# Adding each step's probabilities in two halves, and moving sums, projections and value products in the order

## The reference

```python
q = (x @ wq_w.T + wq_b).reshape(b, t, H, HD)
k1, v1 = (x @ wk_w.T + wk_b), (x @ wv_w.T + wv_b)      # one head of 32
scores = jnp.einsum('bqhd,bkd->bhqk', q, k1) / jnp.sqrt(jnp.float32(HD))
weights = jax.nn.softmax(jnp.where(causal, scores, -jnp.inf), axis=-1)
attn = jnp.einsum('bhqk,bkd->bqhd', weights, v1).reshape(b, t, H * HD)
x = _layernorm(x + (attn @ wo_w.T + wo_b))
x_scale = FP8_MAX / jnp.maximum(jnp.max(jnp.abs(x2)), EPS)   # w_scale alike
out = clip(x2 * x_scale) @ clip(weight * w_scale) * (1.0 / (x_scale * w_scale))
x = _layernorm(x + out)
```

## Time and profile before

| what | value |
|---|---|
| median of three runs | 2414.62 us |
| profiled execution | 2413.82 us |
| its span (first to last instruction) | 2411.7 us |
| mean granted TensorE clock | 0.991 |
| attention, batch 0 to last value product | 417.8 to about 1989 us |
| batches 1 to 19, no projection | 422.6 to 528.3 us |
| batches 20 to 271 | 528.3 to 1987 us |

### The profile page before, as it was taken

How to read it: one execution, slowest core, us unless ns; L and a number is a source line. 1 busy time by engine, 2 the same in 40 slices (tenths; PEclk the granted TensorE clock), 3 DMA queues, 4 the chain that set the end, 5 groups by cost and what they waited for, 6 DMA issues and landing times.

```text
span 2411.7 us, 34838 instructions
## 1 busy us (share of the span) xinstructions
PE 2338.3 (97%) x13933; PEld 1484.1 (62%) x13933; DVE 1809.0 (75%) x1466; ACT 1346.0 (56%) x1459; POOL 640.1 (27%) x381
## 2 busy tenths in 40 slices
PE   8999998899999999999999999999999998999998
PEld 6887776345555555555555555555555556888887
DVE  6455447798889888889899988988888885444444
ACT  3433334777777777777777777777777772000000
POOL 1000002011323222232222222322223222666663
PEclk9999999999999999999999999999999999999999
DMA  7777875211311222121211122122212222222221
GB/s 279 258 266 258 285 261 198 41 36 47 78 45 45 64 55 60 45 67 45 67 45 45 54 69 56 45 54 58 67 45 58 61 71 107 87 87 89 93 87 61
DMA packets 160249, 231.60 MB, mean 96 GB/s; under 512 B 9614, under 2 KB 109934, under 8 KB 158318
## 3 DMA queue, kind: packets, MB, share of 16 engines
q1 hardware_dynamic: 136494, 178.27, 25.5%
q10 hardware_dynamic: 23616, 51.39, 5.7%
HBM read 140.50 MB, written 89.13 MB: 95 GB/s over the span
## 4 chain that ended last, share of the span: by engine, by line
PE 71%; DVE 5%; ACT 3%; issue 2%; POOL 1%; DMA 0%; ACTq 0%; DVEq 0%; POOLq 0%
PE bank L1372 20%; PE bank L1384 18%; PE bank L1447 14%; PE bank L1357 13%; ACT prob L821 3%; DVE acc L1118 2%; PE bank L1394 2%; POOL prob L663 1%; PE bank L1437 1%; PE bank L1402 1%; DVE acc L1114 1%; DVE r_den L1073 1%; DVE r_parts L1077 0%; DVE res L1090 0%; DMA wf<-wf_sim_d 0%
## 5 line engine op out<-in xcount | busy, mean ns | idle before, releaser
L821 ACT ACTIVATE prob<-bank 128x1024 f32<-128x1024 f32 x1088 | 1055.8, 1023 | 410.2 <-PE bank L1372 390.2
L1118 DVE TENSOR_TENSOR acc<-acc,prob 128x2048 f32<-128x2048 f32 x420 | 961.1, 2288 | 58.1 <-ACT prob L821 35.1
L1372 PE MATMUL bank<-q_st,keys 98*128 98x512 f32 x2176 | 646.8, 416 | 16.6 <-ACT prob L821 13.2
L1372 PEld LDWEIGHTS bank<-q_st,keys 98*128 98x128 f32 x2176 | 376.2, 189 | 352.7 <-ACT prob L821 259.7
L1384 PE MATMUL bank<-prob,v_t 128*32 128x512 f32 x4352 | 525.8, 601 | 0.0
L663 POOL TENSOR_SCALAR_AFFINE_SELECT prob<-prob 128x1024 f32<-128x1024 f32 x128 | 206.4, 1636 | 743.2 <-ACT prob L821 743.2
L1384 PEld LDWEIGHTS bank<-prob,v_t 128*32 128x32 f32 x4352 | 114.0, 109 | 263.4 <-issue 251.6
L1114 DVE TENSOR_TENSOR acc<-prob 128x2048 f32<-128x2048 f32 x60 | 137.6, 2293 | 118.4 <-ACT prob L821 87.9
L634 POOL TENSOR_SCALAR moments<-moments 128x1 f32<-128x1 f32 x64 | 66.8, 1044 | 596.7 <-DVE moments L878 568.9
L1357 PE MATMUL bank<-wo_hi,att_hi 128*128 128x512 f32 x512 | 209.0, 408 | 14.4 <-issue 11.3
L852 ACT ACTIVATE xs_hi<-bank 128x1024 fp32r<-128x1024 f32 x32 | 32.9, 1029 | 336.3 <-DVE y L883 328.3
(11 more groups left out here) (131 smaller groups left out, 2435.6 us busy)
## 6 DMA issues: line engine op xcount, KB each, us to landing
q_st<-q_hi_d SPq DMA_DIRECT2D x128, 256.0 KB
q_hi_d<-part_hi ACTq DMA_DIRECT2D x64, 256.0 KB, 2.2
q_lo_d<-part_lo ACTq DMA_DIRECT2D x64, 256.0 KB, 2.8
x_row<-x SPq DMA_DIRECT2D x32, 512.0 KB, 3.9
xb_d<-x_row SPq DMA_DIRECT2D x32, 512.0 KB, 3.9
q_st<-q_lo_d SPq DMA_DIRECT2D x64, 256.0 KB
res<-xb_d SPq DMA_DIRECT2D x32, 512.0 KB, 5.5
x_d<-res SPq DMA_DIRECT2D x32, 512.0 KB, 2.7
```

What stands on the lines that cost most here:

```text
L821: nc.scalar.activation(prob[:, s % SLOTS, 2 * p:2 * p + 2], bank[:, 2 * p:2 * p + 2], ACT.Exp, scale=SCALE).then_inc(p_done, 1)
L1118: nc.vector.tensor_tensor(acc[:, n % 2], acc[:, n % 2], new, ALU.add).then_inc(acc_done, 1)
L1372: last = nc.tensor.matmul(bank[:, g].rearrange("p (a n) -> p a n", n=P), keys[:, k // QT, k % QT * P:(k % QT + 1) * P], queries[:, :, g], ...
```

## The change

VectorE's add of a step becomes two adds of 128x1024, each behind its own exponential, and `acc_done` counts two a step. The residual sums stand ahead of the adds of their step. In `places` the projection ranges, sums and what follows them come two steps (one batch) later, with four ranges of three batches for the next to last pair. Statistics go to the first group that begins at or after SUM1, and deviation, scaling and maximum are placed from there. In a batch without a slice of projection, the value product of step 2u-2 stands between the two scores.

```diff
@@ -311,29 +311,36 @@
         LAST_GROUP = len(groups) - 1
         WF_ORDER = (6, 7, 4, 5, 0, 1, 2, 3)
 
+        SPLIT, HALF0, HALF0_END, SUM0, HALF1, HALF1_END, SUM1, DEVIATION, SCALE_ROW, LARGEST, STATISTICS = range(11)
+
         def places(q):
 
 
 
             p, second = divmod(q, 2)
             if p < len(pairs) - 2:
-                names = (13, 22, 28, 28, 30, 38, 38, 39, 44, 45) if second else (4, 6, 12, 12, 14, 20, 20, 22, 27, 28)
+                names = (13, 24, 30, 30, 32, 40, 40, 41, 46, 47) if second else (4, 8, 14, 14, 16, 22, 22, 23, 28, 29)
                 base = (p + 1) * PAIR
             elif p == len(pairs) - 2:
-                names = (11, 18, 22, 22, 24, 30, 30, 31, END, END) if second else (4, 6, 10, 10, 12, 16, 16, 18, 22, 23)
+                names = (11, 20, 24, 24, 26, 30, 30, 31, END, END) if second else (4, 8, 12, 12, 14, 18, 18, 19, 23, 24)
                 base = (p + 1) * PAIR
             else:
                 names = (END,) * 10 if second else (31,) + (END,) * 9
                 base = p * PAIR
-            return [base + at for at in names]
+            at = [base + at for at in names]
+            statistics = at[SUM1]
+            if p < len(pairs) - 2:
+                statistics = min(first for first in begins if first >= at[SUM1])
+                at[DEVIATION], at[SCALE_ROW] = statistics + 1, statistics + 6
+                at[LARGEST] = min([first for first in begins if 0 <= first - statistics - 7 <= 4] + [statistics + 7])
+            return at + [statistics]
 
         def at_place(name):
 
             return {places(q)[name]: q for q in range(TILES) if places(q)[name] < STEPS}
 
-        SPLIT, HALF0, HALF0_END, SUM0, HALF1, HALF1_END, SUM1, DEVIATION, SCALE_ROW, LARGEST = range(10)
         split_at, sum0_at, sum1_at, deviation_at = at_place(SPLIT), at_place(SUM0), at_place(SUM1), at_place(DEVIATION)
-        scale_at, largest_at = at_place(SCALE_ROW), at_place(LARGEST)
+        scale_at, largest_at, statistics_at = at_place(SCALE_ROW), at_place(LARGEST), at_place(STATISTICS)
         fillers = {}
         for q in range(LAST_A):
             at = places(q)
@@ -815,7 +822,7 @@
             for s in range(STEPS):
                 if s < STEPS:
                     act.wait_ge(pv_done, s + 1)
-                    act.wait_ge(acc_done, s + 1)
+                    act.wait_ge(acc_done, 2 * (s + 1))
                     for p in range(2):
                         act.wait_ge(s_done, 2 * s + p + 2)
                         nc.scalar.activation(prob[:, s % SLOTS, 2 * p:2 * p + 2], bank[:, 2 * p:2 * p + 2], ACT.Exp, scale=SCALE).then_inc(p_done, 1)
@@ -885,7 +892,7 @@
             dve.sem_inc(wf_tile_read, 1)
             dve.sem_inc(norm_read, 2)
             dve.sem_inc(lo_cut, 2)
-            dve.sem_inc(acc_done, SLOTS)
+            dve.sem_inc(acc_done, 2 * SLOTS)
             dve.sem_inc(att_ready, 2)
             dve.sem_inc(t_lo, 2)
             dve.sem_inc(f_read, 4)
@@ -1100,6 +1107,10 @@
                 nc.vector.tensor_tensor(att_lo[q % 2][:], att[:, q % TILES_KEPT], att_hi[q % 2][:].bitcast(F32), ALU.subtract).then_inc(att_cut, 1)
 
             for s in range(STEPS):
+                if s in sum0_at:
+                    add_residual(sum0_at[s], 0)
+                if s in sum1_at:
+                    add_residual(sum1_at[s], 1)
                 if s < STEPS:
                     n, t = steps[s]
                     new = prob[:, s % SLOTS]
@@ -1107,27 +1118,27 @@
                         dve.wait_ge(den_done, n + 1)
                     if t == 0 and lengths[n] == 1:
                         dve.wait_ge(masked, 2 * n + 2)
-                        nc.vector.tensor_copy(acc[:, n % 2], new).then_inc(acc_done, 1)
+                        nc.vector.tensor_copy(acc[:, n % 2], new).then_inc(acc_done, 2)
                     elif t == 1:
                         dve.wait_ge(masked, 2 * n + 2)
-                        dve.wait_ge(p_done, 2 * s + 4)
-                        nc.vector.tensor_tensor(acc[:, n % 2], prob[:, (s - 1) % SLOTS], new, ALU.add).then_inc(acc_done, 2)
+                        for p in range(2):
+                            heads = slice(2 * p, 2 * p + 2)
+                            dve.wait_ge(p_done, 2 * s + p + 3)
+                            nc.vector.tensor_tensor(acc[:, n % 2, heads], prob[:, (s - 1) % SLOTS, heads], new[:, heads], ALU.add).then_inc(acc_done, 2 * p + 1)
                     elif t > 1:
-                        dve.wait_ge(p_done, 2 * s + 4)
-                        dve.wait_ge(acc_done, s + SLOTS)
-                        nc.vector.tensor_tensor(acc[:, n % 2], acc[:, n % 2], new, ALU.add).then_inc(acc_done, 1)
-                if s in sum0_at:
-                    add_residual(sum0_at[s], 0)
-                if s in sum1_at:
-                    add_residual(sum1_at[s], 1)
+                        for p in range(2):
+                            heads = slice(2 * p, 2 * p + 2)
+                            dve.wait_ge(p_done, 2 * s + p + 3)
+                            dve.wait_ge(acc_done, 2 * (s + SLOTS) + p - 1)
+                            nc.vector.tensor_tensor(acc[:, n % 2, heads], acc[:, n % 2, heads], new[:, heads], ALU.add).then_inc(acc_done, 1)
                 if s % 2 == 0 and s // 2 in group_of_den:
                     invert(group_of_den[s // 2])
                 if s % 2 == 0 and s // 2 - 1 in group_of_den:
                     normalise_group(group_of_den[s // 2 - 1])
                 if s in split_at:
                     lower_attended(split_at[s])
-                if s in sum1_at:
-                    q = sum1_at[s]
+                if s in statistics_at:
+                    q = statistics_at[s]
                     dve.wait_ge(y_read, 2 * q + 2)
                     moments_of(res[:, q % 2], stats[:, q % 2], moments[:, q % 2], ln1, q * LN)
                 if s in largest_at:
@@ -1388,7 +1399,7 @@
             def denominators(n):
 
                 pe.wait_ge(att_ready, n + 2)
-                pe.wait_ge(acc_done, begins[n] + lengths[n] + SLOTS)
+                pe.wait_ge(acc_done, 2 * (begins[n] + lengths[n] + SLOTS))
                 for g in range(HG):
                     for c in range(QT):
                         last = nc.tensor.matmul(bank[c * HD:(c + 1) * HD, DEN_BANK, 0:P], head_col[:, g], acc[:, n % 2, g, c * P:(c + 1) * P],
@@ -1414,9 +1425,13 @@
             for u in range(BATCHES):
                 scores(2 * u)
                 between(u)
+                single = u >= 1 and u not in fillers
+                if single:
+                    weigh_values(2 * u - 2)
                 scores(2 * u + 1)
+                if u >= 1 and not single:
+                    weigh_values(2 * u - 2)
                 if u >= 1:
-                    weigh_values(2 * u - 2)
                     weigh_values(2 * u - 1)
             weigh_values(STEPS - 2)
             weigh_values(STEPS - 1)
```

## The result

The changed kernel takes 2397.89 us (median of four runs, 2397.3 to 2399.34), the kernel before 2414.32 in the same comparison. The ratio is 0.9932, 95% interval 0.9921 to 0.9944: 16.4 us faster. Forecast were 2387.5 us and 27 us less, in a range of 2374 to 2406. The sign is right and the time is inside the range, but the gain is 0.6 of what was forecast, and the reasons are further from the forecast than the number is.

The account below looks back on a forecast made before the run. Instruction order bounds batches 1 to 19; later TensorE is full, with stalls on VectorE's late results. Terms -13 - 0.5 - 13 - 5 + 3 + 1.5 = -27 take 2413.8 to 2386.8 us, 2387.5 as median; range 2374 to 2406.

Parts of the forecast that it names:

- (a): Batches 1 to 20 and 271: value product ahead of the second scores fills TensorE's wait; -13 us, and -0.5 for batch 271.
- the sum by VectorE's work: Batches 1 to 20: VectorE may set the rate; 94 us of work plus start and waits gives 98 to 101.
- The check by TensorE alone: Batches 1 to 20 by TensorE only: 16 at 4.43, four with denominators at 5.25, 2 for the clock; 94 us.
- (b): Adds in halves: 1.14 us each, 2.28 a step against 2.38; in the projection part the gain costs and gives nothing.
- rival E: Slower: a half add costs over 1.33 us, VectorE bounds the projection part, about 2440 us; chance 0.11.
- (c): Projections one batch later: `att_lo` is ready in time, 14 stalls ahead of projections go; -13 us.
- (d): Residual ahead of the adds, next half a batch later: four waits for residuals and two smaller ones go; -5 us.
- (e): Costs: eight projection halves end in batches with denominators, so inverses come late for spreads, +3 us; projection slices fall differently, +1.5.
- Slices: Projection matmuls spread differently over batches of the next to last pair and three more denominator batches; +1.5 us.
- A: The forecast as summed holds: 2376 to 2398 us; chance 0.58.
- B: Smaller gain: halves start 1.22 us apart, or waiting residuals leave VectorE short; 2397 to 2408 us; chance 0.17.
- B's second part: Projection part: up to 1.7 us of waiting at 56 residuals leaves VectorE short, so stalls partly return.

Follow-up runs that it names:

- places_only: Kernel before with later projections, sums ahead of adds and moved statistics, but whole adds and the old order of value products: 2418.9 us, ratio 1.0010.
- whole_adds: Changed kernel with whole adds again in place of half adds: 2411.4 us, ratio 0.9977.
- pool_later: Changed kernel with GpSimd's first statistic, and that tile's scaling and maximum, two steps later, behind the mask of step 68: 2390.1 us, ratio 0.9902.
- sum_by_den: Changed kernel with the residual sum behind the adds again in steps where a group's inverse is due: 2386.8 us, ratio 0.9887.
- halves_only: Kernel before with only the adds split in halves: 2403.4 us, ratio 0.9937.

## Why the prediction was right or wrong, point by point

**What bounds the kernel: right.** Order in the plain part, a full TensorE with short stalls in the rest. The floor of 5.35 for six matmuls stayed.

**(a) The value product: right in size, with a term that wasn't in the sum.** Forecast -13 for batches 1 to 20, measured -12.6; plain batch forecast 4.43, measured 4.5. 6.9 us come with the product alone and 12.6 with the half adds too, since half adds let VectorE keep up with the faster batches, as the sum by VectorE's work said. But some 3.1 of the 12.6 us are clock: that the first batch's 7.52 us "stays" was wrong, and the second slow stretch was left to the range (up to 2 us). Without them the gain would be 9.5 us, still in the -8 to -18. The check by TensorE alone has a slip: 4.43 + 1.15 is 5.58 and not 5.25 for a batch with denominators (measured 5.38 to 5.65), and it counts the four batches with a spread as plain, which took 5.27 to 5.78. The forecast didn't rest on it.

**(b) Half adds: the price right, the worth wrong.** 1.13 us from start to start against 1.14 taken; rival E, a half that costs over 1.33 us, is dead. By the page VectorE: DVE Perf Modes of the Trainium skill (section The TRN2 errata — SBUF-src ops pay a fixed extra latency per instruction) each half should last 1.22 us (an estimate), and it does (L1133, 1221 ns); but VectorE's busy time rose by 16.7 us and not by 75, since halves that follow each other overlap. The step that failed is the sentence that a gain there "costs and gives nothing", since VectorE isn't the bound. It priced throughput only. The halves take 0.92 us off the wait at the head of each chain of residual, cut and inverse, and TensorE waited at the end of those chains: -10.1 us in batches 21 to 270, alone, and 15 without GpSimd's first use.

**(c) and (d), stalls that go: right that they go, wrong to whom they belong.** No wait ahead of a projection is left after, as forecast, and long time in batches without denominators or spread fell from 15.8 to 1.6 us. But most of it had two cures in the same change. Places and sums without halves remove these stalls too (places_only has about 1.4 us of them left) and lose as much elsewhere, by the waits shown for whole_adds and GpSimd's pause. The forecast counted -18 for them and had nothing against them but (e).

**(e) Costs: the mechanism right, the size too small.** The sum ahead of the adds makes the inverse late where a half ends in a batch with denominators. Forecast eight cases, 0.7 each at most, taken as 3; there are nine, at 0.87, 7.8 us in all. The reason given for halving it, that in many the add is the second step of a group and late anyway, was wrong: that add waits for its sum as well. Slices: +1.5 forecast, +2.1 by the usual lengths.

**What the prediction didn't have.** GpSimd's first use, 5.5 us. The text let GpSimd's root move along without a cost and looked at SP's queue but not at GpSimd's own, where the next group's mask now stood behind the first statistic. The trace of before held it: there the configuration change is issued at 578.2 and the first statistic starts at 584.96, with nothing queued behind it. And 2.8 us behind the last value product (422.7 us before, 425.5 after). There the last denominators wait 1.26 us for an add, where they waited 0.09. The rest is TensorE's clock in the following 70 us, and that is not the change's doing. Busy time of these 70 us, after, before and in pool_later, whose code there is that of after:

```profile
1969.03:2039.03 70.00, 58.80 (x296) 46.83 (x289) 42.43 (x55) 16.70 (x17) 20.28 (x16) 0.90 0.29 108
```
```profile
1987.06:2057.06 70.00, 59.60 (x308) 47.66 (x301) 42.73 (x53) 16.17 (x16) 22.88 (x18) 0.93 0.30 111
```
```profile
1961.37:2031.37 70.00, 58.66 (x304) 46.93 (x297) 43.60 (x56) 16.68 (x17) 22.07 (x18) 0.93 0.31 113
```

pool_later has the same wait of 1.27 us, but the clock of before, and takes 423.6 us to the end (sum_by_den too). So about 0.9 of the 2.8 us are the change's.

Together: -27 forecast; +4.8 for (e), +5.5 for GpSimd, +0.6 for slices, +2.8 at the end and +1.2 at the start make -12.1; the stalls that went were 21.2 us and not 18, which makes -15.3, and the profiled execution shows -15.2. Of these terms the 1.2 us at the start and 1.9 at the end lie between executions of the same code, so that 3 us of the missing gain are in this pair of profiles and not in the change. The agreement to 0.1 us says little of each term.

**The rivals.** The time, 2397.9, lies on the border of A and B (2398 and 2397), but not by B's mechanism: halves don't start 1.22 apart, and VectorE isn't short. B's second part, residuals that wait for `y_done`, comes nearest.

## What to carry to other kernels

Where an engine has idle time, ask not only what an edit does to its load but when its work starts: splitting an instruction so that its first part begins behind the first of two inputs moved the add behind it by 0.92 us, and was worth 12.7 us on an engine that was 88% busy in that stretch and not the bound. When a step is moved on an in-order queue, list what then stands behind it, on every engine it touches, and look there for a first use that pauses; and when a sum or copy is put ahead of other work, look for the steps in which that other work has a deadline of its own.

## What the runs showed of the hardware that was not expected

GpSimd pauses once, at its first small arithmetic instruction after other kinds, behind a configuration change, and not again after that: 8.29 us in the changed kernel, 7.41 in pool_later, 8.7 to 10.1 in the four kernels with spare instructions. In the kernel before and in halves_only the time from the configuration change to that instruction is 6.7 and 7.2 us, and in halves_only the instruction's own record then reads 9.15 us. Why the size differs is open.

TensorE's longest waits mostly cost more than themselves. The nine longest in batches 21 to 270 of all the kernels are 2.1 to 3.7 us, and behind eight of them TensorE runs at 1.2 GHz for a while: in the changed kernel the batch with the wait of 2.41 us has a granted clock of 0.83 and loses another 1.6 us. Behind the ninth, 2.42 us in sum_by_den at the same place, the clock stays at 1.00.

GpSimd's small instructions last as long as what VectorE does beside them lets them. The same 128x1 instruction, over the projection part (min/median/max ns), before and in halves_only, which changed VectorE's adds alone and left this instruction in its place:

```profile
L634 POOL TENSOR_SCALAR moments<-moments x27: 508/2070/2075, 585.0 to 1854.7; 128x1 f32<-128x1 f32 x27
```
```profile
L634 POOL TENSOR_SCALAR moments<-moments x28: 716/1003/9152, 581.3 to 1893.3; 128x1 f32<-128x1 f32 x28
```

Before, it starts beside a whole add of 2.29 us and lasts 2.07; in halves_only it starts beside a half of 1.22 us and lasts 1.00. After, where the statistics have moved, it mostly stands in a gap of VectorE, and its median is 0.24:

```profile
L641 POOL TENSOR_SCALAR moments<-moments x28: 232/243/1316, 604.5 to 1897.5; 128x1 f32<-128x1 f32 x28
```

So its length follows the VectorE instruction that it starts beside. The masks (128x1024) went from 1636 ns on the mean before to 1378 in halves_only and 1332 after.
